# A whole-array filler matmul in front of each head's key scores, in layer 2 and in four turns of layer 0

## What is computed

```python
scores  = einsum('bhqd,bhkd->bhqk', q, k) / sqrt(8)
weights = softmax(scores, axis=-1)
out     = einsum('bhqk,bhkd->bhqd', weights, v)
```

## Time and profile before

| | us |
|---|---|
| median of 3 runs (2122.66 to 2132.72) | 2122.93 |
| the profiled execution, its own time | 2128.31 |
| its span, first to last instruction | 2125.4 |
| PE busy | 1610.8 (76%) |
| DVE busy | 1238.8 (58%) |
| ACT busy | 765.9 (36%) |
| POOL busy | 379.4 (18%) |

### The profile page before, as it was taken

How to read it: one execution, slowest core, us unless ns; L and a number is a source line. 1 busy time by engine, 2 the same in 40 slices (tenths; PEclk the granted TensorE clock), 3 DMA queues, 4 the chain that set the end, 5 groups by cost and what they waited for, 6 DMA issues and landing times.

```text
span 2125.4 us, 44203 instructions
## 1 busy us (share of the span) xinstructions
PE 1610.8 (76%) x12567; PEld 1046.8 (49%) x12567; DVE 1238.8 (58%) x3512; ACT 765.9 (36%) x1723; POOL 379.4 (18%) x488
## 2 busy tenths in 40 slices
PE   3245899999932559988997368888882688888888
PEld 3122566666610358877886134555551244554554
DVE  5544566666631765665566455666662667766664
ACT  2012454445411222332223035555551324444444
POOL 1265011101164101111112510000006200000000
PEclk9855899999955568898886569999995579999999
DMA  7012454455411000000000123333331011111110
GB/s 227 30 56 66 148 171 151 149 170 171 131 54 34 1 0 1 0 0 0 0 0 0 52 78 107 109 114 120 118 100 48 3 50 41 40 39 47 40 46 14
DMA packets 133278, 144.90 MB, mean 68 GB/s; under 512 B 15001, under 2 KB 114130, under 8 KB 132946
## 3 DMA queue, kind: packets, MB, share of 16 engines
q1 hardware_dynamic: 100946, 106.20, 16.1%
q10 hardware_dynamic: 26112, 25.17, 3.9%
q0 software_dynamic: 6144, 12.60, 1.9%
HBM read 104.65 MB, written 39.52 MB: 68 GB/s over the span
## 4 chain that ended last, share of the span: by engine, by line
PE 47%; DVE 21%; issue 14%; another core or an unknown queue 6%; DMA 6%; SPq 2%; ACT 2%; DVEq 1%; POOL 1%; ACTq 0%; POOLq 0%
PE pO L694 6%; PE pT_ L557 5%; PE pH L584 5%; DVE X L1285 4%; PE pH L500 4%; PE pY L592 4%; PE pS L642 3%; DVE mx L1246 3%; PE pS L664 2%; DMA xsb<-sorted_x 2%; PE pT_ L490 2%; DMA stk<-packed_qk 2%; PE pT_ L555 2%; DVE stk L1252 2%
## 5 line engine op out<-in xcount | busy, mean ns | idle before, releaser
L804 ACT ACTIVATE pex<-pT_ 128x512 f32<-128x512 f32 (+1 forms) x768 | 426.5, 562 | 680.6 <-PE pT_ L557 308.4
L1246 DVE TENSOR_REDUCE mx<-pS 128x2 f32<-128x512 f32 x512 | 347.6, 689 | 228.3 <-PE pS L540 110.0
L557 PE MATMUL pT_<-stk 32*128 32x256 f16 x1024 | 203.3, 295 | 122.6 <-DVE mx L1246 35.5
L540 PE MATMUL pS<-stk 32*128 32x256 f16 x1024 | 214.2, 299 | 42.5 <-DMA stk<-packed_qk 19.3
L694 PE MATMUL pO<-pex,va 128*9 128x256 f32 (+1 forms) x3072 | 211.7, 397 | 2.0 <-ACT pex L804 2.0
L797 ACT ACTIVATE wb<-pH,b 128x256 f32<-128x256 f32 x256 | 107.3, 470 | 273.0 <-PE pH L500 273.0
L890 POOL TENSOR_TENSOR qk<-qkf,qk 128x512 f16<-128x512 f32 x48 | 55.4, 1155 | 731.8 <-DVE qk L1218 369.2
L557 PEld LDWEIGHTS pT_<-stk 32*128 32x128 f16 x1024 | 55.3, 94 | 239.4 <-issue 101.2
L500 PE MATMUL pH<-XT,w 128*128 (+1 forms) x512 | 147.7, 416 | 0.0
L1252 DVE SCALAR_TENSOR_TENSOR stk<-pS,stk 128x512 f16<-128x512 f32 x96 | 66.4, 692 | 134.7 <-PE pS L664 88.9
L807 ACT ACTIVATE xts<-pO 128x256 f32<-128x256 f32 x192 | 73.8, 384 | 183.1 <-PE pO L694 112.3
(11 more groups left out here) (195 smaller groups left out, 2827.2 us busy)
## 6 DMA issues: line engine op xcount, KB each, us to landing
wb<-in_w SPq DMA_DIRECT2D x111, 514.0 KB, 4.0
stk<-packed_qk ACTq DMA_DIRECT2D x96, 256.0 KB, 2.7
packed_qk<-qk SPq DMA_DIRECT2D x144, 128.0 KB, 2.0
xsb<-sorted_x SPq DMA_DIRECT2D x111, 64.0 KB, 3.5
sorted_y<-ysb SPq DMA_DIRECT2D x111, 64.0 KB, 3.2
sorted_x<-wb SPq DMA_DIRECT2D x2, 2048.0 KB, 13.6
w<-in_w SPq DMA_DIRECT2D x2, 1024.0 KB
out<-X SPq DMA_DIRECT2D x16, 128.0 KB, 1.8
```

Of the source, the lines that this page charges most:

```text
L540: return pe.matmul(bank[:, part * T:(part + 1) * T], stk[rows, side, j, part * P:(part + 1) * P], stk[rows, side, j, T:2 * T], start=True, ...
L557: return pe.matmul(bank[:, part * T:(part + 1) * T], key, stk[rows, side, j, 0:T], start=True, stop=True)
L804: act.activation(pex[:, k % 8, 0:n], bank[:, 0:n], ACT.Exp).then_inc(s("T_free"), 1)
L1246: ins = dve.tensor_reduce(mx[:, :, j, col], bank.rearrange("p (c n) -> p c n", c=2), AX.X, ALU.max)
```

## The change

PE gets one more matmul in a T step: the bfloat16 identity as weights (128 x 128) against a mask row repeated four times, so 128 partitions x 512 columns, into the whole `pT_` bank. It stands behind the wait for that bank and in front of the wait for the `pS` bank of the paired S step. The key scores then overwrite the bank. It is issued where the layer is 0 or 2 and the turn has fewer than four blocks: all 16 turns of layer 2 that have T steps (256 fillers) and turns 0, 1, 14 and 15 of layer 0 (64 fillers).

```diff
+            def keep_clock(turn, bank):
+
+                if turn.layer in SORTED and blocks_of(turn.layer, turn.n)[1] < 4:
+                    pe.matmul(bank.rearrange("p (c n) -> p c n", c=4), identb[:, :],
+                              maskb[:, 1, None, :].to_broadcast([P, 4, P]), start=True, stop=True)
...
                         key_scores_mask(l, bank)
+                        keep_clock(turn, bank)
                         after = turn.steps[at + 1]
```

## The result

The changed kernel takes 2130.11 us (median of 20 runs) beside 2123.22 for the kernel before in as many runs: 1.004 times as long, 95% interval 1.0021 to 1.0058. The forecast was 2130 us within 2108 to 2150. The difference is inside the 0.5% that was called "same", and its sign is sure. The profiled execution took 2140.45 us, its span is 2138.3: 12.9 us more span than before. Of these some 5 are scatter: this execution lies 10.3 us above its kernel's median, that of before 5.1 above its own.

A forecast was written before the change was run, and what follows sets the result against it. PE was taken to bound the loop of layer 2. Terms 11 - 2 - 2 - 1 + 0 + 1 = +7 us on the median of 2122.9 gave 2130 us, range 2108 to 2150.

The forecast's parts named there:

- Term 1: 13 block turns of layer 2: 26.7 us each, all warm, against 25.87 on the mean, so +11 us.
- the forecast's best case: Loop of layer 2: all 2.5 us of PE's standing take fillers, a turn takes 25.3, loop gains 7 us.
- What a filler costs: Each added 512-column matmul: 0.213 us at 2.4 GHz, 0.43 at 1.2 GHz, its weight load nothing behind a full-array matmul.
- The dips: Clock drops in layer 2's loop: about 2.2 us each; with longer transfers 19 us over 13 turns; fillers prevent them.
- Turn 0 of layer 2: Cold turn with 16 fillers, only the first 8 counting: clock rises some us earlier, -2 us.
- the first rival: Cold ends of the layers: fillers don't lift the clock there, only keep it in the loop; +31 us, 2154, chance 0.22.
- Tail of layer 2: Second half of turn 14 and turn 15, 24 fillers: between cold +5 and warm -6, taken as -2 us.
- Layer 0's start: Up to the projection of turn 1, 24 fillers: between cold +7 and warm -6, taken as 0.
- its turn 14 and tail: Layer 0's last 4 heads of turn 14 and turn 15: -1 us; the first 12 fillers of turn 14: nothing.
- the code term: Written-out turns get 160 more matmuls; longer program may bring one more stall at the gathers: 0 to +8, taken as +1.
- The second: Rival: fillers run where PE would stand anyway, over 3.0 of a loop turn's 4.0 us swallowed; -19 us, 2104, chance 0.17.
- The third: Rival: loop dips return every other turn because the L616 token wait remains; +13 on the forecast, 2143 us, chance 0.08.

The follow-up runs named there:

- the loop alone: Kernel before with the added matmuls only in turns 1 to 13 of layer 2 (208 of 320): 2026.63 us against 2014.79, 1.0059.
- tokens first: Kernel before, no added matmuls, SP issues a block's 64 KB of tokens ahead of its 514 KB of weights: 1999.86 us against 2014.49, 0.9913.
- the last experiment: Kernel before with tokens issued ahead of weights in layer 2 only, added matmuls only in turns without blocks of layers 0 and 2: 2100.7 us, 0.9878.
- the eight heads without waits: Kernel before with added matmuls only in layer 2's block turns at heads 2, 3, 4, 8, 9, 11, 13, 14: 2017.33 us, before at 2012.0.

## Why the prediction came out

**Term 1, the loop: sign and mechanism right, size too large by the profiles.** Forecast +11 us with 26.7 us a turn, all warm and without a wait at L616. The pair of traces shows +4.9 with 26.24, all warm, no such wait. With the three loops without fillers in it and weights first (336.3, 333.7, 336.1: mean 335.4) against the three with sixteen (341.2, 343.2, 342.5: mean 342.3) it is +7. The runs of the loop alone, +11.8 us on medians, would even fit the forecast, but the loop of its profile, 343.2, is only 8 above that mean of 335.4; where the rest lies isn't shown. The error of 0.46 us a turn is in what is swallowed. Of the gross 4.0 us (16 x 0.213 + 0.4 + 0.2) I let 1.71 be swallowed; 26.24 - 24.4 = 1.84 was paid, so 2.16 was swallowed, nearly all of the 2.5 that PE stood. That also shows a slip in the forecast's best case: even with all 2.5 us filled, the 0.6 for the lost overlap and the changes stays, so a turn would take 25.9 us and the loop would gain nothing, not 7 us. One piece that I missed: behind the two heads after the bias matmul PE waited 0.16 us for `ysb`, and the place cost 1.71 - 0.87 = 0.84 us and not 1.03 (bias matmul to the next block's second matrix: 1420.46 to 1422.17 above, 1438.73 to 1439.60 in the trace of before). The gross price holds: with tokens first PE stands 2.1 us a turn (23.90 - 21.82), after the change 0.2 (26.30 - 26.10), so 1.9 are swallowed and 26.24 - 24.0 = 2.2 paid, 4.1 in all.

**What a filler costs: right.** 0.32 us from its start to the scores was 2 x 0.107 and 0.1 for the change. The point drawn from the Trainium skill (TensorEngine Tiling (Array Packing), section Tiling Modes) holds as it was weighed: the change costs its 0.1 us, and not at every head. Charged at all heads it would have cost 33 us more, and the loop did not.

**The dips: right that they go, and what brings most of them is now shown.** The prediction priced a dip at 2.2 us from two kinds of turns and took from layer 3 that fillers prevent it. They do, but the clock hangs on the waits: the stand for tokens at L616 stood ahead of all 13 dips in the two loops of before, and the fillers and tokens first, which each take it away, left none there but one in the last experiment. Fillers do so at 2 us a turn, whether by delaying PE or by filling the other waits beside it, which the runs don't part; tokens first does it with no filler and without that price. The forecast's "all that a steady clock could give back is 19 us" came out near, 335.4 to 315.9 is 19.5, but partly by chance: the 24.4 us of its warm turn still held a stand of some 0.5 us at L616, with tokens first a turn takes 24.1, and in return the first turn of that loop, still cold, took 27.0.

**The ends.** Turn 0 of layer 2: forecast -2, measured +0.8 in the pair, where the first part stayed at 0.50 to its end, as the first rival had it. The stall behind it stayed, as the chain of waits of the kernel after shows for the packed queries:

```profile
1264.24 3.81 DMA stk<-packed_qk
```

Tail of layer 2: -2 and measured -2.7, with a clock of 0.89. Layer 0's start: 0, measured +2.1 with turn 1; its turn 14 and tail: -1, measured +2.1, all of it ahead of turn 15. Together that is +2.3 in the pair (0.8 - 2.7 + 2.1 + 2.1) where the forecast had -4 with the code term. In the group without the stands the same fillers alone gave -7.4 us on medians. Whether the ends are worth less beside the stands is not shown: no run there has them alone, the +2.3 comes from two single executions, and the whole change costs 6.9 us on medians with the stands and 4.6 without, with overlapping intervals.

**Code.** Forecast +1. The stretch behind the gathers, turn 14 of layer 0, grew by 2.1 us (98.9 to 101.0); the longest stand in the chain of waits of the kernel after is

```profile
653.59 34.32 another core or an unknown queue
```

against 30.88. The instruction queue moved 0.66 MB and not 0.62. That the two belong together isn't shown: in the groups without stands the same longer program had no loss there (30.5 and 31.3 us).

**What I had no term for.** The block turns of layer 0, where nothing was changed, took 5.7 us longer in the profiled run, and the sum over the touched stretches is +7.2 of the span's +12.9. This is the scatter of single executions: turns 2 to 13 of layer 0 took 377.9 to 384.6 us with weights first, by dips that come at some turn or not, as in the kernel after's turns 6 (none) and 5 (one):

```profile
349.60:380.40 30.80, 29.02 (x264) 19.48 (x266) 19.37 (x49) 15.15 (x32) 3.37 (x4) 1.00 0.48 151
315.70:349.60 33.90, 31.87 (x264) 20.78 (x266) 19.51 (x49) 15.09 (x32) 3.37 (x4) 0.90 0.47 142
```

The median's +6.9 meets the forecast's +7, and that it meets it so closely is luck. By the profiles two errors offset each other: the loop was over-priced by 4 to 6 us and the ends came out some 6 worse. By the medians of the parts, +11.8 and -7.4 where the forecast had +11 and -4, there was less to offset. The runs don't decide between the two readings.

**The rivals.** The first (the ends stay cold, +31) had the clock of the ends half right and the price wrong: no stretch cost its cold price. Turn 0 of layer 2 shows why for itself: its eight fillers, 3.4 us at half clock, went into the 2.7 us that PE stood there, and the 13.4 us became 13.5. The second (all swallowed, -19) had its swallowing nearly right for the waits, 2.2 of 2.5 us, but not its point of decision: more than 3.0 of 4.0 could not be swallowed where PE stands 2.5, and the eight heads without waits pay 1.4 us a turn. The rule of the Trainium skill beside it (TensorE: Matmul & The Clock Gate, Part 1), followed to its end, would have had all cold stretches warm; the rows show 0.50 to 0.96 there with PE busy in 13.49 of 13.5 us at 0.50. The third (dips stay) is refuted: none in 341.2 us.

## What to carry to other kernels

Before feeding a clock, look at what stands ahead of each dip: here a wait of 0.4 to 2.2 us for a small transfer issued behind a large one, and swapping the two issues gave 14.6 us (0.9913) where 208 fillers in the same loop lost 11.8. In this loop a filler was nearly free only in front of an instruction that PE would wait for anyway; its price elsewhere was its columns, plus the overlap that it breaks. Price a change of this kind stretch by stretch, since gain at the ends and loss in the loop can cancel to a difference that no total explains.

## What the runs showed of the hardware

The same program has two surroundings that differ by 110 us. Turn 14 of layer 0 takes 98.9 us with stands of up to 30.88 us on all engines while POOL issues gathers, or 31.3 us without them, where the kernel before takes 2012 to 2015 us in place of 2123. No kernel of this case turns one into the other; a group of runs has one of them throughout. The chip alone is not the cause, for the same one had both in two groups (before at 2014.49 and at 2124.89). Between the two profiles of the kernel before, 17.0 us of the difference lie in turns 0 and 1 of layer 0, 67.6 in its turn 14 and 36.7 in turn 14 of layer 2, the stretches of POOL's scatters and gathers. What it is stays open.

Each of the seven dips in the loop of before was 3.4 us at half clock, with PE not busy in 0.8 to 2.7 of the 3.4 us ahead (3.4 less the busy time of such windows) and a token wait among them. The wait is not enough by itself: eight of the 21 in the two loops of before had no dip behind them; the 2.1 us that PE stands in every turn of 23.9 us with tokens first, spread over the turn, brought none from turn to turn.

A quarter-array matmul of 512 columns and one of 256 columns in other rows start within 0.01 us of each other (1328.92 and 1328.93); behind a filler over the whole array the scores start only 0.32 us later.

PE busy in 13.49 of 13.5 us did not lift the clock in turn 0 of layer 2: it stood at 0.50 throughout.
